# A decoder kernel: two attention stages begin their steps on half of the tokens, and identity products stand at other places

## The reference

```
x = x + attn(_layernorm(x)); x = x + xattn(_layernorm(x), ctx); x = x + ffn(_layernorm(x))
```

## Time and profile before

| | us |
|---|---|
| median of 3 runs | 1002.85 |
| lowest and highest | 1002.51, 1004.27 |
| profiled execution | 1003.97 |
| its span | 1002.1 |
| TensorE busy in it | 940.9 (94%) |
| VectorE busy in it | 607.2 (61%) |
| ScalarE busy in it | 489.9 (49%) |
| GpSimd busy in it | 346.9 (35%) |

### The profile page before, as it was taken

The page is one execution under the profiler, slowest core; times in us unless marked ns, Lnnn a source line. Parts: engine busy times, 40 slices in busy tenths (PEclk is TensorE's granted clock), DMA queues, the critical chain, the costliest instruction groups (busy, mean ns, idle before and its releaser), DMA issues.

```text
span 1002.1 us, 17365 instructions
## 1 busy us (share of the span) xinstructions
PE 940.9 (94%) x6700; PEld 707.9 (71%) x6700; DVE 607.2 (61%) x1289; ACT 489.9 (49%) x1120; POOL 346.9 (35%) x439
## 2 busy tenths in 40 slices
PE   7999999999898899999999999999999989899999
PEld 4556889985575689994433347777768876678998
DVE  7786743468876652230899986544666467853222
ACT  2564444447635554434766634434435547733443
POOL 4752089955317300000366853222120026410000
PEclk9799999999999999999999999999999999999999
DMA  6700011100010001103000001000000000001011
GB/s 121 218 10 12 1 43 43 33 22 2 2 43 1 12 30 34 43 11 126 0 1 0 1 0 44 1 1 1 1 1 1 1 2 2 4 9 37 28 43 33
DMA packets 32180, 25.49 MB, mean 25 GB/s; under 512 B 3612, under 2 KB 28384, under 8 KB 31843
## 3 DMA queue, kind: packets, MB, share of 16 engines
q1 hardware_dynamic: 32099, 24.39, 8.6%
HBM read 23.85 MB, written 0.52 MB: 24 GB/s over the span
## 4 chain that ended last, share of the span: by engine, by line
PE 67%; DVE 22%; issue 6%; POOL 2%; ACT 2%; POOLq 0%; DVEq 0%; ACTq 0%
PE banks L911 19%; PE banks L888 14%; DVE work L1529 5%; PE banks L368 4%; DVE banks L1522 4%; PE banks L359 3%; PE banks L1741 3%; PE banks L1733 3%; DVE work L533 2%; PE banks L391 2%; PE banks L1755 2%; PE banks L1792 2%; PE banks L1780 2%; PE banks L41 1%; DVE work L525 1%
## 5 line engine op out<-in xcount | busy, mean ns | idle before, releaser
L967 ACT ACTIVATE work<-banks,keep 128x512 f32<-128x512 f32 x236 | 157.0, 688 | 174.0 <-PE banks L888 173.9
L911 PEld LDWEIGHTS banks<-keep,work 128*128 128x128 f32 x1888 | 220.8, 192 | 6.1 <-ACT work L967 0.7
L911 PE MATMUL banks<-keep,work 128*128 128x128 f32 x1888 | 222.7, 275 | 0.6 <-ACT work L967 0.6
L1057 DVE SCALAR_TENSOR_TENSOR keep<-banks,keep 128x128 f32<-128x128 f32 x256 | 72.4, 344 | 177.0 <-PE banks L911 176.3
L888 PE MATMUL banks<-rounded 128*128 128x512 f32 x672 | 172.8, 404 | 3.5 <-DVE rounded L1026 2.0
L888 PEld LDWEIGHTS banks<-rounded 128*128 128x128 f32 x672 | 122.1, 190 | 30.6 <-issue 4.1
L700 ACT ACTIVATE work<-banks,work 128x128 f32<-128x128 f32 (+1 forms) x448 | 121.7, 387 | 36.0 <-DVE work L525 28.6
L150 POOL TENSOR_TENSOR keep<-keep 128x4 f32<-128x4 f32 x26 | 26.7, 1028 | 229.8 <-DVE keep L129 211.7
L1595 POOL TENSOR_TENSOR work<-work,keep 128x1024 f32<-128x1024 f32 x31 | 73.3, 2369 | 62.2 <-DVE work L1529 62.2
L525 DVE TENSOR_REDUCE work<-banks 128x8 f32<-128x1024 f32 (+1 forms) x64 | 68.9, 1077 | 35.5 <-PE banks L359 32.4
L368 PE MATMUL banks<-keep,work 128*128 128x128 f32 (+1 forms) x448 | 64.0, 284 | 10.9 <-DVE work L533 10.7
(11 more groups left out here) (292 smaller groups left out, 1393.0 us busy)
## 6 DMA issues: line engine op xcount, KB each, us to landing
keep<-in_L_ffn_w_dram SPq DMA_DIRECT2D x32, 256.0 KB, 3.1
keep<-in_L_ffn_W_dram SPq DMA_DIRECT2D x16, 256.0 KB, 3.0
keep<-in_L_xattn_Wkv_dram SPq DMA_DIRECT2D x1, 2048.0 KB, 9.0
keep<-in_L_ffn_expert_w_dram SPq DMA_DIRECT2D x8, 128.0 KB, 2.3
keep<-in_L_ffn_expert_w_dram SPq DMA_DIRECT2D x1, 1024.0 KB, 5.6
keep<-in_L_attn_conv_w_dram SPq DMA_DIRECT2D x1, 1024.0 KB, 7.6
keep<-in_ctx_dram SPq DMA_DIRECT2D x1, 960.0 KB, 8.3
keep<-in_x_dram SPq DMA_DIRECT2D x2, 256.0 KB, 3.5
```

Source lines behind the costliest of these rows:

```text
L911: m = pe.matmul(k.ps[:, self.bank(n, j), j * P:(j + 1) * P], k.hT[n % 2][:, c, j * P:(j + 1) * P], w2[c], start=c == 0 and self.kind != "d ...
L967: act.activation(k.hT[n % 2][:, c, :], k.ps[:, c, :], self.func, bias=bias, scale=scale)\
L1057: ins = dve.scalar_tensor_tensor(acc[:, t, :], k.ps[:, self.bank(n, j), j * P:(j + 1) * P], k.w[:, 8 * t + e:8 * t + e + 1], acc[:, t, :], ...
```

## The change

Self and context attention: maxima 0 go ahead of the second half's statistics (self, through the new argument `last` of `Experts.vector`) or ahead of the second half's adding (context, in `dense_sums`). The second half is normalised in step 1, transposed in step 2 and copied in step 3; its power on GpSimd stands behind the key blocks of sequence 1. Between score product 1 and step 0 stand 8 identity products in self (13 before, eight of them between the transposes) and 6 in context (14 before); context has 8 more at the start of step 1. Context no longer waits for `taps_ready` on TensorE. "packed" keeps its order.

"gate" gets 4 identity products behind the first half's routing logits. Layer 0's bias product takes the identity and all 128 rows of the bias tile, in which each row is the bias, in place of one row of ones and one row.

```diff
 # Attention.tensor
         if self.kind == "packed":
             pe.wait_ge(*self.behind.acc_done.upto(self.behind.items))
-        if self.kind == "context":
-            pe.wait_ge(*self.behind.taps_ready.upto(2))
-        if self.kind != "rope":
             spin(k, pe, PT0, 3)
             self.turn.tensor_half(pe, 1, PT0, 2)
-            spin(k, pe, PT0, {"self": 2, "context": 3, "packed": 5}[self.kind])
+            spin(k, pe, PT0, 5)
+        if self.kind == "self":
+            spin(k, pe, MB, 8)
+        if self.kind == "context":
+            spin(k, pe, OB, 6)
         for s in range(self.STEPS + 4):
+            if s == 1 and self.kind == "context":
+                spin(k, pe, OB, 8)
             if s + 2 < self.STEPS:
                 self.scores(pe, s + 2)
...
             if 1 <= s <= self.STEPS:
                 self.times_v(pe, s - 1)
+            if s == 2 and not self.proj:
+                self.turn.tensor_half(pe, 1)
 # Attention.vector
-        self.maxima(dve, 0)
+        if self.proj:
+            self.maxima(dve, 0)
         if self.setup:
             self.setup.vector_edges(dve)
-        if self.kind != "rope":
+        if self.kind == "packed":
             self.norm.normal(dve, 1)
         self.maxima(dve, 1)
...
             if s < self.STEPS:
                 self.turned_weights(dve, s)
+            if s == 1 and not self.proj:
+                self.norm.normal(dve, 1)
 # Attention.pool
-        if self.kind != "rope":
+        if self.kind == "packed":
             self.norm.power(pool, 1)
         self.values_of(pool, 0)
...
             self.query_key_parts(pool, c, 1)
             self.key_blocks(pool, 1)
+        if not self.proj:
+            self.norm.power(pool, 1)
 # Attention.scalar
-        if self.kind != "rope":
+        if self.kind == "packed":
             self.turn.scalar_half(act, 1)
         self.weights(act, 1)
...
             if s < self.STEPS:
                 self.weights(act, s)
+            if s == 3 and not self.proj:
+                self.turn.scalar_half(act, 1)
 # Experts.tensor
                 elif self.routed:
                     self.route_logits(pe, 0)
+                if self.kind == "gate":
+                    spin(k, pe, PT0 + 1, 4)
 # Experts.vector(self, dve, after=None, done=None, last=None)
                 dve.wait_ge(*self.acc_done.upto(n + 1))
+                if h and last is not None:
+                    last(dve)
                 token_stats(k, dve, k.x, range(4 * h, 4 * h + 4))
 # Depool.tensor_pooled
-            pe.matmul(k.ps[:, self.banks[h], :], k.ones[0:1, :], bcast(k.wide["b_in0"][0:1], 1, 4), start=True, stop=True)
+            pe.matmul(k.ps[:, self.banks[h], :], k.ident, bcast(k.wide["b_in0"], 1, 4), start=True, stop=True)
 # dense_sums
                 l1_after.centre(dve, h)
+                if h:
+                    l1_cross.maxima(dve, 0)
                 l1_after.add(dve, h, n6)
 # vector
-            l0_ffn.vector(dve, n3, done=beside_relu)
+            l0_ffn.vector(dve, n3, done=beside_relu, last=lambda dve: l1_attn.maxima(dve, 0))
```

More of the change, by code:

```diff
@@ L987, in split_x, with vector @@
         self.split(dve, self.k.dchain, self.k.xnT, self.x_high, self.x_low, h * HALF).then_inc(self.x_split.sem, 1)
-    def vector(self, dve, after=None, done=None):
+    def vector(self, dve, after=None, done=None, last=None):
         k, c = self.k, self.k.dchain
@@ L2518, in decoder @@
         l2_mamba = Mamba(k, n8, t8)
-        l1_cross.behind = l2_mamba
         n9 = Norm(k)
```

## The result

| | before | after |
|---|---|---|
| median, us | 1002.68 | 994.85 |
| lowest, highest | 999.51, 1005.68 | 992.99, 1005.72 |
| executions | 6 | 6 |
| ratio, 95% interval | | 0.9936, 0.9909 to 0.9963 |
| profiled execution, its span | 1003.97, 1002.1 | 1005.72, 1003.9 |

The change gains 7.8 us; 995.2 was forecast. The total is close, but two things that decide it pull in opposite directions: one is missing in the prediction, and the other stands there only as a rival with 0.06.

The account below looks back on a forecast made before the run. TensorE was taken as the bound, with two thirds of the last-ending chain; savings count where it waits or runs slow. Terms 1.3 + 1.0 + 3.5 + 1.9 = 7.7 us off 1002.85 gave 995.2 us, range 992.9 to 999.0.

Parts of the forecast that it names:

- The slower rival: Self and context attention steps start at half clock and stay there, up to 6.8 us lost each, 1008.8 us; chance 0.06.
- one-row product: Pooled rows, layer 0: identity bias product keeps the clock up behind it; 1.3 us saved, bounds 0 and 1.6.
- self attention: Handover: score product 3 starts 2.15 us earlier, part given back by product 7; 1.0 us kept, ends 0 and 2.1.
- context attention: Handover: score product 3 at 301.0 against 307.06, shrinking by product 7; 3.5 us kept, bounds 2.3 to 4.3.
- last expert layer: Four identity products fill a 1.08 us wait and keep the clock: 4.62 to 2.75, 1.9 us, bounds 0 and 1.9.
- The four terms: Savings at pooled rows, self attention, context attention and last expert layer: 1.3 + 1.0 + 3.5 + 1.9 = 7.7 us.
- the step that failed: First attention: 26.4 to 40.0 us at clock 0.50 with TensorE busy, said to have nothing ahead but steps.
- clock unmoved: Rival: clock falls at 98 and 903 for another reason, so first and fourth terms are 0; 998.3 us, chance 0.10.
- the second rival: Second half becomes the wait in both attentions: self keeps nothing, context 2.3; 997.3 us, chance 0.10.
- the 0.5 that was set as a bound: Context attention sign: TensorE never idle over 0.5 us; wrong if a score product waits longer for a maximum behind the normalising.
- 0.50 shows within the steps: Attention steps: granted clock 0.50 appearing there was named as a sign that the prediction is wrong.

Follow-up runs that it names:

- e2: Kernel after with the one-row bias product put back and without the gate's four identity products; median 995.84 us, ratio 0.9959.
- e7: Kernel after plus two identity products ahead of the weights' transposes in every odd step of context attention; median 992.08 us, ratio 0.9895.
- e3: Kernel before with only layer 0's bias product changed to the identity on 128 rows; median 999.65 us, ratio 0.998.
- e4: Kernel before with only the gate's four identity products in the last expert layer; median 1000.88 us, ratio 0.9977.
- e9: Kernel before, old order, with identity bias product, gate's fill and longer fills ahead of the second half's transposes; median 996.48 us, ratio 0.9949.
- e12: Kernel before again, unedited, for its profile; one execution, 1004.14 us.
- e5: Kernel before with self attention's new handover and the first attention's five identity products; median 997.62 us, ratio 0.9941.
- e6: Kernel after without context attention's 14 identity products; median 1009.6 us, ratio 1.0061.
- e1: Kernel after again, unedited; median 995.07 us over 12 executions, ratio 0.9948.

## Why the prediction was right and where it was wrong

By its own steps, with what the traces measured in like places:

| term | predicted | measured | |
|---|---|---|---|
| one-row product | 1.3 | 1.4 | 14.15 to 12.73, from L2134's 16 products (93.89) to layer one |
| self attention | 1.0 | 1.5 | product 1 to 7: 19.07 to 17.60 |
| context attention | 3.5 | 2.8 | 44.85 to 42.06 where the clock holds (e2) |
| last expert layer | 1.9 | 1.6 | transposes to layer two: 8.23 to 6.66 |
| sum | 7.7 | 7.3 | |
| first attention | no term | 5.3 | 95.87 to 90.61 |
| context attention at 0.50 | a rival | -13.3 | in 4 of 18 executions |

The four terms held to within 0.5 in their sum. That the medians came out 0.35 from the forecast is luck all the same. e7, with the same edits and a held clock, has a span of 989.8, which is 12.3 below the 1002.1 of before: the four terms (7.25) and the first attention (5.26), less 0.4 for its fills, leave 12.1. So with the clock held the change gains 12, and not 7.7. After's executions at 1.00 stand there too (992.0), but its median is 2.9 above them, and the median of before stands 1.3 below its profiled execution. 12.3 less these two is 8.1, near the 7.8 measured. The clock that after loses again hides most of the missing term. Not every execution of before has its long first stretch either: eight of the 66, at 996.7 to 998.8, have mean clocks of 0.997 and 0.998, which leave no room for 13.7 us; no profile caught one.

**First attention, the step that failed.** The prediction read the stretch from 26.4 to 40 at 0.50 and said that there was nothing ahead of it but steps. Its own row of the first microsecond, 26.00:27.00, has TensorE at 0.00: there was a wait of 1.66 us, in TensorE's row for L2076, and the change fills it. All five profiles without that fill have the wait (before, e3, e4, e9, e12), and four of them the fall: 13.7, 3.4, 3.4 and 13.7 us (e4 none). None of the nine other profiles has it. The fill was not run by itself, so its own size isn't separated from chance in the clock; e5 comes closest, and e4 shows what the place takes when the clock happens to hold.

**One-row product.** Right in size (1.4 for 1.3), and mostly by its mechanism, 1.0 clock and 0.4 the form itself (e5): wherever the row of ones stood, four of five profiles show the clock falling behind it (before, e2, e4, e12; not e5), and none of the nine with the identity does. At 903 it is five of five profiles without the gate's fill (before, e2, e3, e5, e12) and none of the nine with it. So the rival "clock unmoved" is refuted at 98 and at 903 alike. The fall at 98 comes with TensorE busy, so by the Trainium skill, TensorE: Matmul & The Clock Gate, section Why this matters for your kernels, which ties mid-kernel drops to idle stretches, it wasn't to be expected; the runs bear out the row and not that rule.

**Self attention.** The normalising was priced at 1.11 to 2.30 and took 1.52. Of the 1.95 that product 3 gained, 1.5 was kept to the end and not 1.0: a quarter was given back and not half, and the second rival, by which the second half becomes the wait and nothing is kept, is refuted. From product 1 to context attention's product 1 it is 81.23 us against 82.67, so nothing was given back later.

**Context attention.** The term of 3.5 was mis-sized. Product 3 came 6.0 earlier, as said, and 2.8 was left at product 7 (16.54 to 13.73), at the layer behind 2.8 again (44.85 to 42.06). Of these 1.55 are order and 1.2 clock. The miss lies ahead of product 5, which came 9.24 behind product 1 and not 8.4. VectorE's adding was carried with its 1.15, but beside GpSimd's key blocks it takes 1.90. In e2, VectorE:

```profile
292.94 1.90 DVE L1241 SCALAR_TENSOR_TENSOR keep<-keep 128x128 f32<-128x128 f32 x4
```

 So the power ends 6.3 behind product 1 where 5.4 was forecast, and the third key block with it. The waits at products 4 and 5 were 0.36 and 0.39, under the 0.5 that was set as a bound.

**Last expert layer.** Mis-sized by mixing two views: 4.62 was a row of TensorE and 2.75 a stretch of the chain. Row against row it is 4.62 to 3.04.

**The slower rival** had the right mechanism and the wrong condition. "The steps start at half clock and stay there" was given 0.06 and a price of at most 6.8 us per stage, taken from a stretch of 13.6 us; so one stage alone would have meant no change. One stage stayed low for 41 us, at 13.3 us, and did so in 4 of 18 executions. Its argument against this, fills in the first waits and new waits under 0.5 us, did not hold: both were as said, and the clock fell. "0.50 shows within the steps", the sign by which the prediction would be wrong, did show in its first profile. The median doesn't show it, since it is the smaller part of the executions; without the fills it would have been every execution (e6), and the change a loss.

Not settled: what makes an execution of after fall at 299 or not. The same instructions with the same idle times did both.

## What to carry to other kernels

Read every idle time of TensorE ahead of a low stretch, the first stage's too, before saying what a change will do; and don't price a fall of the clock by the length of another one: it lasted 3.4 us in some places and 41 or 58 in others. When a new order shortens a wait, keep identity products in what is left of it: fourteen of them were the difference between 0.6% slower and 0.6% faster here, and one or two more in each odd step, with its 0.4 us wait, left no long execution among 23, at a cost of 0.1 to 0.4 us (one product alone stands on five executions). Time such a change over a dozen executions and look at each one's mean clock, since a median hides one execution in five that is over 10 us longer.

## What the runs showed of the hardware

- Steps of context attention at 1.2 GHz didn't come back to 2.4 by being busy: 40.98 busy us in 41.10 (after), 55.62 in 58 (e6). They consist of products over 32 and 96 rows, transposes, and products with the values into 32 columns. Which of these keeps the clock low, no run separates.
- Within one kernel the time follows the low stretches, at less than half of their length: 41 us at half clock cost 13.3 us (after against e2), 13.7 us cost 5.2 (before against e4).
- The same instructions take the fall in one execution and not in another: e1 between 991.7 and 1006.6, e4's first attention against before's with an identical 1.66 us wait.
- The 8 products behind four one-row records take 1.16 at full clock (e5) and 1.05 behind four records of the identity (after).
